# Eight gathered tiles under way in place of four, and sums of y dealt out at other steps, in a two-layer graph kernel

## The reference

```python
# layer 0: attention over the neighbours
h = relu(layernorm(x))
H = h @ W.T + b
s, r = H @ a_s, H @ a_r
e = leaky_relu(A * s + A * r.T, 0.2)
x = x + softmax(where(A > 0, e, -9e15), axis=1) @ H
# layer 1: sum over the neighbours, then a maximum over the neighbours
h = relu(layernorm(x))
out = relu(adj @ (h @ weight) + bias)
x = x + max over the neighbours j of out[j]
```

## Time and profile before

| | |
|---|---|
| median of 3 runs | 2443.19 us (2442.29 to 2444.61) |
| span of the profiled execution, first to last instruction | 2797.4 us |
| profiled span above the median | 354.2 us (14.5%) |
| busy in the span: POOL / DVE / PE / ACT | 1589.9 / 1436.7 / 953.5 / 453.3 us |
| stage A / B / C in the profiled execution | 0 to 1414 / 1414 to 1830 / 1830 to 2797 us |

### The profile page before, as it was taken

The page is one execution under the profiler, slowest core; times in us unless marked ns, Lnnn a source line. Parts: engine busy times, 40 slices in busy tenths (PEclk is TensorE's granted clock), DMA queues, the critical chain, the costliest instruction groups (busy, mean ns, idle before and its releaser), DMA issues.

```text
span 2797.4 us, 18967 instructions
## 1 busy us (share of the span) xinstructions
PE 953.5 (34%) x4466; PEld 535.6 (19%) x4534; DVE 1436.7 (51%) x3301; ACT 453.3 (16%) x1519; POOL 1589.9 (57%) x1616
## 2 busy tenths in 40 slices
PE   3664155525245536433648997600000000000000
PEld 1431044213123213223513442300000000000000
DVE  6888677855344434444255543535546554341132
ACT  1631145302133214523400000000000000000000
POOL 0102745443664654576463564677777777657776
PEclk8987577767667767756869997855555555555555
DMA  9999667888567879732532231152242112112221
GB/s 363 405 383 373 199 228 280 311 221 322 186 226 253 303 265 367 262 81 64 139 92 61 59 79 32 47 132 53 59 66 62 46 47 47 40 39 53 54 55 41
DMA packets 155983, 447.42 MB, mean 160 GB/s; under 512 B 34557, under 2 KB 81459, under 8 KB 122970
## 3 DMA queue, kind: packets, MB, share of 16 engines
q1 hardware_dynamic: 80506, 311.94, 29.4%
q0 software_dynamic: 53184, 114.44, 17.2%
q10 hardware_dynamic: 22176, 19.77, 2.3%
HBM read 408.06 MB, written 37.95 MB: 159 GB/s over the span
## 4 chain that ended last, share of the span: by engine, by line
POOL 21%; issue 17%; another core or an unknown queue 16%; DVE 15%; PE 14%; DVEq 8%; SPq 3%; DMA 3%; ACT 2%; ACTq 0%; POOLq 0%
POOL rec_all L683 10%; PE psV L1115 10%; POOL ring L683 9%; DVE words L1243 2%; DVEq L1242 2%; DMA a_buf<-in_adj 2%; POOL out L689 2%; DVE words L1234 2%; DVE words L1238 2%; DVEq L1237 2%; SPq L412 2%; DVE rec_all L1267 1%; PE psV L942 1%; PE psH L998 1%
## 5 line engine op out<-in xcount | busy, mean ns | idle before, releaser
L611 POOL DMA_INDIRECT ring<-h_table,srec x518 | 507.1, 979 | 301.6 <-issue 169.2
L683 POOL DMA_INDIRECT rec_all<-p_table,srec x354 | 360.9, 1019 | 114.4 <-issue 108.9
L942 PE MATMUL psV<-a_buf,bit_ident 128*128 128x512 bf16 x1024 | 314.4, 472 | 240.6 <-DMA a_buf<-in_adj 156.1
L1125 PE MATMUL psH<-ones_row,flag_col 128*1 128x1 f32 x2 | 0.2, 164 | 767.1 <-issue 767.1
L683 POOL DMA_INDIRECT ring<-p_table,srec x191 | 194.5, 1019 | 59.2 <-issue 59.2
L646 POOL DMA_INDIRECT ring<-y_table,srec x198 | 192.0, 970 | 62.7 <-issue 62.7
L998 PE MATMUL psH<-ring,ident 128*128 128x128 f32 x1036 | 163.7, 320 | 143.6 <-remote 51.3
L1115 PE MATMUL psV<-rec_all,a_buf 128*128 128x512 bf16 x869 | 199.9, 384 | 14.3 <-issue 13.3
L1353 DVE TENSOR_REDUCE squares<-rec_all 128x128 f32<-128x640 f32 (+14 forms) x51 | 82.2, 1612 | 227.0 <-DMA rec_all<-p_table,srec 209.7
L942 PEld LDWEIGHTS psV<-a_buf,bit_ident 128*128 128x128 bf16 x1024 | 114.5, 114 | 422.6 <-issue 240.5
L998 PEld LDWEIGHTS psH<-ring,ident 128*128 128x128 f32 x1036 | 155.4, 233 | 154.6 <-issue 144.9
(11 more groups left out here) (232 smaller groups left out, 2131.7 us busy)
## 6 DMA issues: line engine op xcount, KB each, us to landing
a_buf<-in_adj SPq DMA_DIRECT2D x256, 1024.0 KB
ring<-h_table,srec POOLq DMA_INDIRECT x518
trec<-records ACTq DMA_DIRECT2D x63, 128.5 KB
packed<-wbuf ACTq DMA_DIRECT2D x28, 256.0 KB
a_buf<-packed SPq DMA_DIRECT2D x7, 1024.0 KB
rec_all<-p_table,srec POOLq DMA_INDIRECT x354
h_table<-stage POOLq DMA_DIRECT2D x16, 258.0 KB, 7.7
a_buf<-r_row SPq DMA_DIRECT2D x1, 4096.0 KB
```

Source lines behind the costliest of these rows:

```text
L611: pool.indirect_dma_start(ring[:, A_AT[q] + j, :], None, h_table, bass.IndirectOffsetOnAxis(srec_u[g][:, i, LIST + j:LIST + j + 1], 0)).th ...
L683: pool.indirect_dma_start(ring[:, at + j, 0:D] if at < RING else side[:, at - RING + j, :], None, p_table, bass.IndirectOffsetOnAxis(slot, ...
L942: last = pe.matmul(psV[n % 2][:, h * BANK:(h + 1) * BANK].rearrange("p (g n) -> p g n", n=P), bit_ident[:, k, :], rows[:, :, k, :], start= ...
```

## The change

`BUFS` goes from 4 to 8, for the gathers of all three stages, their semaphores and the plan of places of stage C. The scatters of p stand seven tiles behind the gathers in place of three (`LAG_P`), and count on one semaphore in place of four. The step of a sum is its count of POOL instructions (plus 8) divided by 5, in place of times 9/32.

```diff
-BUFS = 4
+BUFS = 8
+LAG_P = 7
...
 def sums_behind(step):
-    return [m for m in range(len(Y_SLOTS)) if min((sum(Y_SLOTS[:m + 1]) + m + 8) * 9 // 32, DENSE_BATCHES * BLOCKS - 1) == step]
+    return [m for m in range(len(Y_SLOTS)) if min((sum(Y_SLOTS[:m + 1]) + m + 8) // 5, DENSE_BATCHES * BLOCKS - 1) == step]
...
-        s_pscat = [sem(f"s_pscat{i}") for i in range(BUFS)]
+        s_pscat = sem("s_pscat")
...
-                                        y_save[:, m, :], None).then_inc(s_pscat[m % BUFS], 16)
+                                        y_save[:, m, :], None).then_inc(s_pscat, 16)
...
             for m in range(len(Y_SLOTS)):
                 gather_y(m)
-                if m >= 3:
-                    scatter_p(m - 3)
-            for m in range(len(Y_SLOTS) - 3, len(Y_SLOTS)):
+                if m >= LAG_P:
+                    scatter_p(m - LAG_P)
+            for m in range(len(Y_SLOTS) - LAG_P, len(Y_SLOTS)):
                 scatter_p(m)
...
-            for m in range(BUFS):
-                pool.wait_ge(s_pscat[m], 16 * (len(Y_SLOTS) // BUFS))
+            pool.wait_ge(s_pscat, 16 * len(Y_SLOTS))
```

## The result

| | kernel before | the change |
|---|---|---|
| median | 2442.29 us (2439.16 to 2444.61, 9 runs) | 2449.37 us (2445.73 to 2453.45, 9 runs) |
| ratio | | 1.003, 95% interval 1.0021 to 1.0038 |
| profiled execution: span | 2797.4 us | 2447.6 us |
| stage A / B / C of the profiled execution | 1414 / 416 / 968 us | 1217.3 / 342.3 / 888.0 us |

The change makes the kernel slower by 7 us (5 to 9 by the interval). The forecast was 11 us faster, 2432. The time is that of the second rival (+6, 2449), just inside the upper end of the range (2450), and the sign is the other one.

The account below looks back on a forecast made before the run. The bound changes by stage: POOL in C, POOL's waits in A, PE and POOL's tail in B. Only B's term counted, -11 us, A, C and the semaphore nothing: 2443.2 - 11 = 2432 us, range 2423 to 2450.

Parts of the forecast that it names:

- the second rival: Recorded POOL prices hold in timed runs, 1.277 us per instruction: stage B +6 us, 2449, slower; chance 0.17.
- Two clocks, the recorded and the timed: Whole kernel: splits recorded span minus timed median into 79 us (B), 170 (A) and 105 over POOL instructions, 0.084 each.
- t = 1.19: Predicted timed price in us of one POOL instruction, from 1.277 recorded less 0.084; bounds 1.02 and 1.277.
- 194t - 241.8: Stage B: change in when C begins if POOL is slower than its allotment, t its price per instruction; -11 us forecast.
- the 354 us: Whole kernel: recorded span over the timed median, 354.2 us, which the prediction ascribed to the recorder.
- The waits of a gather for a score: Stage A: 36.2 us of recorded POOL waits that eight in flight might remove; costed at nothing, bound -36 us.
- The 32.7 us of waits in C: Stage C: POOL's waits for DVE stay and eight in flight gains nothing; bounds -5 to +5 us.
- The fourth rival: No change, 2443: t between 1.222 and 1.272, or stage B's tail hidden by the last batch's store; chance 0.20.
- The first rival: POOL faster than thought, t under 1.158: PE alone ends stage B, gain 13 to 17 us, 2426 to 2430; chance 0.19.
- Slow stretches as the recorder's doing: Stages A and B: PE's half-clock stretches come from recording; without them B would be 79 us shorter.
- rival 3: Slow PE stretches are real, fed in stage B by POOL issuing without pause: +25 to +45 us, near 2478; chance 0.08.

Follow-up runs that it names:

- i1: Sums at a quarter of a step per POOL instruction, four tiles in flight and scatters three behind kept, against the kernel before: 2421.06 us beside 2443.66, ratio 0.9907.
- k1: Eight tiles in flight and scatters seven behind, sums left at 9/32 of a step, against the kernel before: 2426.05 us beside 2441.39, ratio 0.9933.
- i2: Sums at a fifth of a step, four in flight and scatters three behind kept, against the kernel before: 2458.46 us beside 2443.66, ratio 1.0063.
- k2: Eight in flight, scatters seven behind, sums at a quarter of a step, against the kernel before: 2415.88 us beside 2441.39, ratio 0.9893.

## Why the prediction was wrong

**The failed step** is "Two clocks, the recorded and the timed": "That leaves 354 - 79 - 170 = 105 us, which I spread over the roughly 1250 POOL instructions", and with it t = 1.19. The term of the sum, 194t - 241.8, was right in form; its t measures 1.278, the 1.277 of the recorded rows and not 1.19. With that it gives 194 x 1.278 - 241.8 = +6.1 us, which is rival 2, and the change measured +7.1 (+11.9 when run again). That the sum comes so near is partly luck: by the traces stage B alone became 8.5 to 9.7 us longer, since the one of before is 333.8 and not 336.4, and stages A and C add 0 to 5 in time.

What the 354 us really were, by stage: A 1414 to 1217 (197; I had 170), B 415.9 to 333.8 (82; I had 79), C 967.6 to 888.0 (80). The part for B held. The remainder was in A and C, and in C it can be read. Groups of POOL in stage C, of before:

```profile
L683 POOL DMA_INDIRECT rec_all<-p_table,srec x354 | 360.9, 1019 | 114.4 <-issue 108.9 <-SPq L500 5.2 <-DVEq L1562 0.3
L683 POOL DMA_INDIRECT ring<-p_table,srec x191 | 194.5, 1019 | 59.2 <-issue 59.2
L689 POOL DMA_INDIRECT out<-results,srec x63 | 64.7, 1027 | 50.9 <-DVEq L1562 32.7 <-issue 18.2
```

and of the change:

```profile
L683 POOL DMA_INDIRECT ring<-p_table,srec x315 | 299.9, 952 | 96.0 <-issue 95.7 <-DVEq L1562 0.3
L683 POOL DMA_INDIRECT rec_all<-p_table,srec x230 | 220.5, 959 | 73.4 <-issue 69.5 <-SPq L501 3.7 <-DVEq L1562 0.3
L689 POOL DMA_INDIRECT out<-results,srec x63 | 61.5, 976 | 19.2 <-issue 18.6 <-DVEq L1562 0.6
```

545 gathers went from 1.019 to 0.952 and 0.959 us (35 us), and POOL's wait for DVE from 32.7 to 0.6. So on the slow chip POOL was dearer in C, in some rows (the middle one of them takes 0.948 us there and 0.944 here, and a quiet stretch gave me 1.25 with the gap), but in B, where the price was needed, it was not: the earlier trace rows has 0.970 and 0.988, the change 0.971 and 0.990. Nor was it in A, where the mean gather is 0.979 us in the profile before and 0.980 in that of the change: the 197 us of A were waits (POOL's pauses of over 0.6 us there add up to 353 us in the one and 149 in the other). I took a remainder that I could not place, made it a price, and carried it into a stage whose own rows denied it. The row to go by stood in the front of the argument. I even wrote down the reason against rival 2 ("then A would have to give back all of the missing 275 us"): A gave back 197 of them and C the other 80, C being the stage that I had left at its recorded length for no reason but one quiet stretch.

Point by point, by the list of what would show it:
- POOL's waits for sums under 30 us: 1.2, and the first scatter stands at 1308.94, behind 69 gathers without a pause. Right. But they were worth little: on a 2440 chip they were 33 to begin with.
- No sum behind the last unpack, no gather behind it, C released by SP: right, last sum 1512.48, last unpack 1539.40.
- DVE's waits for y 60 to 110 us: 86.5. PE's gaps for bits: 30.8. Right, and this is the loss.
- Stages A and C within 10 us: by the run with eight in A and C alone, 0 to 5 us in time. The waits of a gather for a score (36.2 us), to which I gave a bound of -36, belonged to the chip: on a 2440 chip there is 0.9 us of them with four in flight (i1) and 0.3 with eight, single gaps of the usual 0.3. There was nothing to gain. The first is i1's row of POOL's waits in A, the second the change's (300 to 1217 us):

```profile
POOL ring L611 <- DVEq L1339: 0.9, 3, 0.3
```

```profile
POOL ring L612 <- DVEq L1339: 0.3, 1, 0.3
```

- The 32.7 us of waits in C "stay": wrong, they belonged to the slow chip.
- The fourth rival's hidden tail: stage C of the run with stage B as before starts 2.1 us behind the start of the iota, on the landing of the last scatter, so the tail is not hidden. The first rival (t under 1.158) falls with t.
- Slow stretches as the recorder's doing: wrong. As a thing of the chip they are real, and rival 3 names what they do there. The change itself was measured on 2440 chips only, so rival 3's price for it (+25 to +45) has no run.

The two parts of the change, each by itself on a 2440 chip: sums' steps +14.8 us, eight in flight -15.3. Their sum is about zero, the change is +7 to +12. They do not add up, because the gain of eight in flight is POOL's and starts to count only when POOL closes the stage; with the sums a fifth apart PE closes it, and all that is left of the gain is four scatters fewer ahead of the last gather: 347.0 to 342.3 and 343.5 us of stage B, where 4t = 5.1.

The best kernel is the change with one number put back above the price: eight in flight with a quarter of a step, 2415.88 us, 25.5 under the kernel before. Where the kernel before takes 2803 to 2812, four in flight with a quarter is the one that gains, and since it is within the interval of the best on the 2440 chips (0.9907 against 0.9893) it is the safer of the two.

## What to carry to other kernels

When one engine's program has to place work for rows that another engine brings, the spacing must be just above the measured price of the one that brings them: at 1.49 us per instruction this kernel has a tail, at 1.06 it starves PE, at 1.32 with a price of 1.28 it has next to nothing of either, and the whole span between is some 40 us. Take that price from rows of the very stage, and when a profiled execution and the timed runs differ by more than a few us, suspect that they were not the same machine before making a price of the difference. A wait that a change removes is worth only what it does at the stage's end: POOL's 33 us of waits for sums went to 12 with eight in flight alone (k1), a gain of 15, and to 0.6 with the sums' steps alone (i2), a loss of 15.

## What the runs showed of the hardware

- The same kernel takes 2441 to 2444 us on some chips and 2803 to 2812 on others. By stage (A, B, C): 1217 / 334 / 888 and 1412 / 418 / 967. On the latter PE falls, in stretches in which POOL issues indirect DMAs without a pause, to rows mostly 1.4 to 2.8 us apart (multiples of 0.70) with no visible releaser, while POOL keeps its pace: 15 matmuls beside 33 POOL instructions in 40 us, where the other chip shows 189 beside 32. Each such stretch ends within 12 us of the start of POOL's next pause. What the cause is stays open; no run here takes it apart.
- So a change can have opposite signs on two chips: eight in flight alone is 0.9933 on one and 1.0105 to 1.0115 on three others.
- An indirect DMA with one row per partition costs POOL 0.97 us in the mean and a gap of 0.30 before the next in stage B, on both kinds of chip, with PE full (k2), starved (the change) or slow (the kernel before): 1.273 and 1.274 us each over 198 gathers, 1.277 to 1.286 with the scatters.
- A starved PE pays twice: 30.8 us of waits for bits in the change's stage B, and granted clocks of 0.91, 0.87, 0.97 and 0.94 in the four stretches of 40 us from 1357 to 1517, where k2 has 1.00. PE's way through the stage, from its first matmul to the start of its last, grew from 301.1 us (k2) to 337.2. Of the 36.1 us, 26.4 are the difference in waits for bits (30.8 against 4.4), and the rest, an estimate by subtraction, is left for the lower clock and the smaller waits.
